# A new order for the same instructions in a one-core transformer block

## The reference

```python
q, k = rope(x @ Wq), rope(x @ Wk); v = x @ Wv          # per head, 8 features
attn = softmax(where(causal, q @ k.T / sqrt(8), -inf)) # (8, 16, 512, 512)
x = layernorm(x + (attn @ v) @ Wo)
logits = x @ router_w.T + experts_bias
rw, sel = top_k(logits, 2); rw = softmax(rw)
cw = (one_hot(sel, 8) * rw[..., None]).sum(1)
eo = silu(x @ w1[e]) * (x @ w3[e])                     # each expert e, 128 -> 256
x = layernorm(x + einsum(cw, eo, w2) + shared expert(x))
```

## Time and profile before

| | |
|---|---|
| median of three runs | 573.11 us (572.95 to 573.9) |
| the profiled execution | 573.02 us |
| its span, first to last instruction | 571.3 us |
| PE busy | 514.5 us (90%) |
| DVE busy | 481.7 us (84%) |
| ACT, POOL busy | 315.5 us, 309.0 us |
| mean granted TensorE clock | 0.957 |

### The profile page before, as it was taken

The page is one execution under the profiler, slowest core; times in us unless marked ns, Lnnn a source line. Parts: engine busy times, 40 slices in busy tenths (PEclk is TensorE's granted clock), DMA queues, the critical chain, the costliest instruction groups (busy, mean ns, idle before and its releaser), DMA issues.

```text
span 571.3 us, 14719 instructions
## 1 busy us (share of the span) xinstructions
PE 514.5 (90%) x4286; PEld 335.9 (59%) x4286; DVE 481.7 (84%) x1981; ACT 315.5 (55%) x744; POOL 309.0 (54%) x517
## 2 busy tenths in 40 slices
PE   7786988889899999999989999999999999999960
PEld 3221344545466646754655687766787979985640
DVE  3797879999999999899987999898994548787993
ACT  3104855676576569676647748575858554542210
POOL 5123645547662257677777447454758836244531
PEclk9875989989999999999999999999999999999995
DMA  6483231308727333642378575664457789980211
GB/s 180 144 260 108 68 123 38 104 26 258 221 68 198 111 102 98 208 126 89 118 210 210 165 201 158 188 175 135 126 153 208 239 264 292 326 262 19 57 41 37
DMA packets 75279, 87.33 MB, mean 153 GB/s; under 512 B 9984, under 2 KB 57984, under 8 KB 75200
## 3 DMA queue, kind: packets, MB, share of 16 engines
q1 hardware_dynamic: 67824, 77.14, 45.8%
q0 software_dynamic: 3584, 7.35, 4.3%
q10 hardware_dynamic: 3792, 1.90, 1.1%
HBM read 64.21 MB, written 20.05 MB: 147 GB/s over the span
## 4 chain that ended last, share of the span: by engine, by line
PE 53%; DVE 16%; issue 9%; SPq 6%; POOL 6%; DMA 5%; ACT 3%; ACTq 0%; DVEq 0%; POOLq 0%
PE ps L1482 13%; PE ps L1388 11%; PE ps L1344 8%; PE ps L1494 8%; DVE sums L1601 4%; PE ps L1504 3%; POOL rows_in L1135 3%; ACT probs L1189 3%; PE ps L1399 2%; DMA xg<-rows_in 1%; POOL probs L1123 1%; SPq L980 1%; PE ps L1466 1%; SPq L969 1%; PE ps L1511 1%
## 5 line engine op out<-in xcount | busy, mean ns | idle before, releaser
L1601 DVE CUSTOM_DVE_ANT_0 sums<-ps,mask_sb 128x384 bf16<-128x384 f32 (+3 forms) x512 | 219.5, 481 | 12.5 <-PE ps L1344 12.2
L1189 ACT ACTIVATE probs<-ps 128x512 f32<-128x512 f32 x320 | 170.8, 611 | 44.7 <-PE ps L1344 42.7
L1123 POOL TENSOR_SCALAR_AFFINE_SELECT probs<-probs 128x256 f32<-128x256 f32 (+1 forms) x320 | 113.4, 364 | 114.3 <-ACT probs L1189 107.5
L1344 PE MATMUL ps<-stack 64*128 64x512 bf16 (+3 forms) x1024 | 117.8, 307 | 16.5 <-DMA stack<-mparts 4.7
L1482 PE MATMUL ps<-xgT,w_tile 128*128 128x128 f32 x672 | 90.3, 280 | 1.9 <-DVE negmax L1601 1.1
L1482 PEld LDWEIGHTS ps<-xgT,w_tile 128*128 128x128 f32 x672 | 80.7, 192 | 9.6 <-issue 6.1
L1344 PEld LDWEIGHTS ps<-stack 64*128 64x128 bf16 x1024 | 40.9, 95 | 74.7 <-issue 17.0
L1388 PE MATMUL ps<-probs,va 128*32 128x512 f32 (+3 forms) x1024 | 80.7, 459 | 2.9 <-POOL probs L1123 1.5
L1145 POOL DMA_INDIRECT yg<-rows_out,slot x56 | 54.0, 965 | 39.5 <-DVE acc L1789 26.2
L1734 DVE SCALAR_TENSOR_TENSOR gate<-th,ps 128x256 f32<-128x256 f32 x116 | 47.1, 414 | 31.2 <-ACT th L1256 30.8
L1256 ACT ACTIVATE th<-ps 128x256 f32<-128x256 f32 x116 | 44.8, 391 | 39.4 <-PE ps L1482 35.9
(11 more groups left out here) (119 smaller groups left out, 683.8 us busy)
## 6 DMA issues: line engine op xcount, KB each, us to landing
w_tile<-in_experts SPq DMA_DIRECT2D x92, 384.0 KB, 4.0
stack<-parts_scratch SPq DMA_DIRECT2D x98, 128.0 KB
parts_scratch<-parts SPq DMA_DIRECT2D x14, 384.0 KB, 3.2
xg<-rows_in SPq DMA_DIRECT2D x18, 256.0 KB, 4.2
rows_out<-y_routed SPq DMA_DIRECT2D x61, 64.0 KB
rows_in<-zeros SPq DMA_DIRECT2D x14, 192.0 KB, 3.8
x_t<-in_x SPq DMA_DIRECT2D x8, 256.0 KB, 2.9
x_r<-in_x SPq DMA_DIRECT2D x8, 256.0 KB
```

Source lines behind the costliest of these rows:

```text
L1123: pool.affine_select(out=area, in_=area, compare_op=ALU.is_ge, fill=0.0, base=0, pattern=pattern, channel_multiplier=-1).then_inc(masked, 1)
L1189: act.activation(probs[:, (s * NB + v) % PRING, :], bank("scores", s, v), ACT.Exp, scale=SCALE)\
L1344: return pe.matmul(into[:, at:at + width], here[:, stationary, at_s:at_s + P], here[:, moving, at_m:at_m + width], start=True, stop=True)
L1601: ins = dve.tensor_tensor_reduce(sums[:, use % 2, at:at + w], bank("max", s, u)[:, at:at + w], mask_sb[:, S - w:S], -1.0, 3.0e38, ALU.add, ...
```

## The change

The instructions are the same on every engine. `LATER` has new numbers throughout, `COST` has new durations, and `plan()` prices a change of the array's shape on PE in both directions and by the kind of step it falls on, where before it priced only the entry into score pairs. Two neighbouring indirect DMAs on POOL are priced too. The core of the diff, with one row of the table for all:

```diff
-LATER = {("act", "T"): (-1464.68, -543.59, -866.19, -282.1, -1194.15, -668.89, -1800.38, -229.23, 713.66, 853.54,
-         -491.16, 267.78),
+LATER = {("act", "T"): (-1975.43, -949.14, 145.58, -2309.33, -522.53, 93.09, -4755.86, -863.93, 520.33, 1162.66,
+         -291.24, -1240.02),
...
-SWITCH = 180
+SWITCH = 95
+CLOSE = 280
+SHAPE = dict(score_pair="rows", max_pair="rows", values="columns")
+AFTER = dict(score_pair=10, max_pair=10, values=0, gate=102, down=102, v=102, out=102, project=102, dense_gate=102, dense_down=102,
+             dense_end=102, router=102, max_rows=13)
...
-                if engine == "pe" and tiled == (kind in ("score_pair", "max_pair")):
+                if engine == "pe" and shape == SHAPE.get(kind, "full"):
                     rank -= AT["stay"]
...
+            if engine == "pool":
+                if kind in ("scatter", "gather") and lines[engine][-2:-1] and lines[engine][-2][0] in ("scatter", "gather"):
+                    taken, lasts = taken + CLOSE, lasts + CLOSE
...
-                if kind in ("score_pair", "max_pair"):
-                    taken, lasts, tiled = (taken, lasts, True) if tiled else (taken + SWITCH, lasts + SWITCH // 2, True)
-                else:
-                    tiled = False
+                if shape != SHAPE.get(kind, "full"):
+                    more = (0 if shape == "columns" else SWITCH) + AFTER.get(kind, 56)
+                    taken, lasts, shape = taken + more, lasts + more, SHAPE.get(kind, "full")
```

More of the change, by code:

```diff
@@ new lines @@
+COST = dict(
+    pe=dict(x_T=(436, 640), project=(1717, 1925), v=(893, 1150), max_rows=(109, 310), values=(2290, 2430), heads_T=(872, 1085),
+            out_T=(436, 640), out=(893, 1095), x1_T=(436, 640), router=(812, 1015), count=(270, 380), rank=(417, 525),
+            T=(109, 310), gate=(893, 1095), down=(446, 650), dense_gate=(1716, 1918), dense_down=(1784, 1988), dense_end=(446, 650),
+            score_pair=(218, 424), max_pair=(218, 424)),
+    act=dict(x_T=(477, 655), rope=(947, 1140), rest=(947, 1140), store_last=(600, 3600), first_act=(600, 2600), v=(494, 655), values=(494, 655),
+             out=(477, 655), x1_T=(477, 655), weights=(95, 230), T=(157, 330), tanh=(272, 416), dense_tanh=(493, 630), down=(165, 360),
+             scores=(478, 665)),
+    dve=dict(project=(1200, 1370), max=(688, 826), max_rows=(1250, 1380), rope=(1160, 1250), rest=(1160, 1250), low=(1160, 1280),
+             heads_T=(728, 868), ln1_stats=(2170, 2335), ln1=(1450, 1600), router=(2080, 2220), weights=(620, 750), count=(533, 665),
+             rank=(1480, 1640), gated=(331, 510), glu=(333, 475), dense_gated=(597, 775), dense_glu=(597, 740), mix=(1036, 1180),
+             mix_end=(386, 400), combine=(2450, 2475), ln2_stats=(1420, 1595), ln2=(1060, 1210)),
+    pool=dict(rope=(2305, 2425), rest=(2090, 2195), low=(2090, 2195), scores=(358, 463), scatter=(993, 4700), gather=(970, 4700),
+              shared_rows=(411, 535), ln1=(1030, 1100), ln2=(1030, 1100)),
+    sp=dict(tables=(1800, 4500), fill=(800, 4500), load_x=(500, 3500), load_residual=(500, 3800), store_parts=(480, 4500), stack=(635, 3400), first=(635, 2700), maxima=(1790, 3400),
+            load_rows=(520, 5000), weight=(800, 4800), store_rows=(590, 3900), out_rows=(480, 3300)))
@@ L227 @@
+SMALL = dict(max=0.888, rope=0.6, rest=0.6, low=0.6, scores=0.7)
 QUARTER = {("dve", "ln2_stats"): 0.36, ("dve", "ln2"): 0.28, ("pool", "ln2"): 0.9, ("sp", "out_rows"): 0.9}
@@ L697, in plan @@
         lines = {engine: [] for engine in COST}
-        ends, holder, held, tiled = {}, [None] * 8, [0] * 8, False
+        ends, holder, held, shape = {}, [None] * 8, [0] * 8, "full"
         bank_of, nth, read, indirect = {}, {}, {}, -HOLD
```

328 lines of the change are left out of this document (159 added, 169 removed).

## The result

The changed kernel takes 583.77 us, median of four runs (583.28 to 584.1), where the old one takes 573.5 on the same chip: ratio 1.0165, 95% interval 1.0122 to 1.0208. The forecast was 569.1, with a range that ended at 575.2. The profiled execution is 583.55 with a span of 581.8, against 573.02 and 571.3: 10.5 us to be found. PE is busy 524.6 us (90%), DVE 483.7 (83%), the mean granted clock is 0.951.

The account below looks back on a forecast made before the run. DVE was taken to bound the kernel first, PE later, DVE's last steps the end. PE's sum 133.1 + 392.2 + 19.7 + 3.0 = 548.0 gained 2.3, the end 1.6: 3.9 off 573.02, 569.1 us; range 564.0 to 575.2.

Parts of the forecast that it names:

- The start: First score pair: maxima issued ahead of stacked loads, pair at 42.2 instead of 46.5, DVE gains 3.0 us (0 to 5).
- a sign that it is wrong: At the start: the forecast is wrong if DVE still waits there for the values step.
- the 3.0: DVE time gained at the start, 3.0 us, taken off DVE's loss at the transposes before sequence 1's projection, giving 133.1.
- The walk: Steps followed from first score pair to second half's max_rows, which comes at 54 to 56 instead of 58.3.
- The handover: DVE hands over to PE at sequence 1's projection transposes, at 133.1; PE then loses 19.7 us, at most 24.7.
- the third rival: All waits shrink: clock stays up at the start, scatters stay covered, 564.1 us; chance 0.22.
- The scatters: Last group, rank to first tile: less PE work and three more POOL masks, PE waits 3.0 us more (0 to 5).
- Shape changes: Array shape changes on PE, 340 instead of 319: 3.2 us more PE work, nearly all behind sequence 2.
- The end: Sequence 6's combine and statistics leave DVE's last stretch: 10.4 us behind PE's end instead of 12.0, 1.6 gained.
- the prediction's own sign for that: Behind 135 us: the forecast is wrong if PE's lost time there is over 27 us.
- The rival of the scatters: Last scatters set the end: rank at 434.0, 574.6 us, slower; decides from a rank later than 432.4; chance 0.22.

Follow-up runs that it names:

- Two runs: New order with rank, last values step and last group's load on SP moved, 1.0127 to the old kernel; new order with all mends together, 1.0075.
- two moves: Old order with first half's maxima ahead of the stacked loads on SP and sequence 0's normalization ahead of a rope step on DVE: 0.9906 to the old kernel.
- the run with the load ahead: New order with rank and last values step mended, plus last group's first loads ahead of sequence 4's output store on SP: 1.0127 to the old kernel.

## Why the prediction was wrong

*The start* held, alone. In the new order DVE's two waits that it aimed at, 1.84 and 3.07, are gone, and 0.84 and 2.39 stand in their place, 1.7 us gained. The 2.39 is a wait behind the second values step, which the prediction had named as a sign that it is wrong. Then new ones of 2.07, 1.03 and 0.50 came at 105 to 136, and the waits of DVE over 0.3 us from 36 us to the transposes sum to 9.3 in both orders. Beyond that DVE worked some 2 us longer on the same instructions (durations between 36 and 138 us less the median of the same instruction: 1.3 in the old kernel, 3.2 in the new), 1.0 of it the cast beside POOL. So the step at the transposes came at 138.3, 5.2 later than forecast: the 3.0 were not kept, and some 2 were added. The walk stopped at max_rows; the price of what follows was not looked for.

*The handover* is the step that failed. "I take 19.7, since from here DVE's excess falls by 3 to 4 us at once and leaves it that much slack": the slack was not there. Of the 19.7, 16.7 were for the way to rank (what the old order lost from 164.12, where 60.6 were lost, to rank); there PE lost 21.9 us, and the old order from the same step had lost 21.6, so what I had as the upper bound was the measure. A count of work done against work done says where an engine must wait at the least. It doesn't say that the other is free behind that point: DVE is busy 19.52 and 19.61 of 20 us in 260 to 280 and 300 to 320, where PE has 18.24 and 18.35, and still 19.68 and 19.78 in 320 to 360. That two level engines lose in small waits on both sides was the argument against the third rival, and it should have gone into the sum. It is a reading of these rows; no run took the small waits away. Nor is it all: in 380 to 420 PE has 18.31 and 18.97 and DVE only 15.65 and 16.18, and PE's longest wait there, 1.06 us, is for a stacked load.

*The scatters* were the right place and the wrong size. Rank came at 438.9, far behind the 432.4 from which that rival decides, and behind its own 434.0: the 9.3 us of work ahead of it were not taken from waits, and 1.9 more were lost. The chain of 36.0 us was measured to the tenth, but by terms that cancel: the first scatter 1.9 later (DVE's combine stands ahead of its rank step, POOL's masks ahead of the scatter), 1.1 for the masks, 2.0 less from last scatter to landing. Not priced: the values step that PE has to run in the meantime, its masks behind the last scatter, its 4.50 at half clock. PE lost 7.3 instead of 4.6. Two runs show that the time from rank to the first tile can be shortened (36.8 and 37.2 us for 38.7); the runs before them show that a step put ahead can push another wait to the front.

*Shape changes*: 3.2 us was the count times the prices, and where PE alone is full the prices hold (220 to 240 of the new kernel: 20.4 us pass for 20.4 counted). The count takes max_rows as a full step, but it runs as 128*32; counted as columns, the changes are 332 and 349, and by the same prices the new order has 2.8 us more instead of 3.2. Taken out between 307 and 450, they gave nothing. The Trainium skill's drain on a mode change (TensorEngine Tiling (Array Packing), Key Properties) is not contradicted; its cost is not the one that ends last there.

*The end* came as worked out, 10.2 us behind PE for a forecast 10.4 (the 0.2 of wake-up in that sum shows in no row: ACT starts 0.04 behind PE's end), and was worth nothing that the times can tell. What the new kernel wins behind PE's end, 1.8 us, it loses ahead of it: from the first tile to the last step before dense_end PE loses 3.2 us, for 1.4 in the old order. The likely reason is that DVE works there without pause in the old kernel, so a combine taken out of its last stretch must be done in one that is as full; no run shows it free of seam waits. The step was measured from the wrong end.

Together: 5.2 at the handover, 5.2 between it and rank, 2.7 at the first tile, 1.8 behind it, less 0.2 at the end: 14.7 until DVE's end, and with what follows it the 14.5 us by which the profiled execution missed. The sign went wrong at the handover, and the prediction's own sign for that came: behind the transposes PE lost 32.4 us, not at most 27. The rival of the scatters had 0.22 and should have had more, since its condition was a rank 4 us later with 9.3 us more work ahead; but its 574.6 was 9 us short as well, since it too kept the gain of 3.0 and the old losses until rank.

## What to carry to other kernels

When an order is moved as a whole, price the chains that PE cannot fill (here rank, scatter, load, first tile) by when they begin and by what is left to run beside them, not by PE's total. An engine found behind at one point is a bound for more than that point: check the busy shares of the stretches after it before calling the rest slack. And try the one edit with a clear wait in the trace by itself first: two moves gave 5.4 us where the new order of all engines lost 10.

## What the runs showed of the hardware

Whether the granted clock falls at a place is in part chance, as far as the rows can tell. The new kernel and the one with fewer shape changes have the same instructions in the same order until 307 us, and in both PE waits 0.46, 0.53 and 0.67 us at 294 to 298. The last of these waits and a stretch behind it, the first pair from the new kernel, the second from the other:

```profile
296.75 0.42 PE L1484 MATMUL ps<-ident_sb,xg 128*128 128x128 f32 x2 [0.67 <-DVE negmax L1619]
...
300.00:305.00 5.00, 5.00 (x56) 2.96 (x57) 4.96 (x18) 4.20 (x9) 4.05 (x6) 1.00 0.21 74
```

```profile
297.88 0.66 PE L1510 MATMUL ps<-ident_sb,xg 128*128 128x128 f32 x2 [0.67 <-DVE negmax L1645]
...
300.00:305.00 5.00, 5.00 (x28) 3.78 (x28) 3.42 (x14) 2.15 (x5) 2.71 (x3) 0.56 0.30 92
```

One stays at 2.4 GHz, the other is at 1.2 GHz for some 7 us, half as many matmuls in the same time, 2.8 us lost. Of the five profiles with this order until there, two show a fall at this place (the other is the run with the load ahead, 0.73 in 295 to 300). The Trainium skill (TensorE: Matmul & The Clock Gate, Part 1: The HAM clock gate) says that the moment of the change at a kernel's start varies from run to run of one kernel; these rows show the like in mid-course. A pair of profiles therefore can't tell a few us; the intervals of the timed runs can.

Some operations on DVE from SBUF to SBUF stood still while POOL ran one: the normalization of four tiles took 3.40 beside POOL's rope sum of 2.35, and 1.56 when moved off it; a cast of 0.22 took 1.22 and ended with POOL's 2.12 at 100.2, while the cast at 98.45, which reads PSUM, kept its 0.28 beside that same step. The Trainium skill (SBUF — State Buffer, SBUF: two separate sides) says that some DVE operations (those in a two-port mode, or with two inputs in SBUF) and GpSimd share a port pair as an exclusive lock: the one that starts first has it for the whole instruction, and the other blocks. The rows agree: the rope sum keeps its 2.35 and DVE takes the delay. That the normalization and the cast ran in such a mode is not in the trace.
